# A graph network of two layers on one core: the last 13 blocks of the second layer as dense products, and one wait per chunk of gathers in the first

## The reference

```python
# first layer
h    = relu(layernorm(x))
ea   = edge_attr @ W_edge.T + b_edge            # (200000, 96)
msg  = relu(h[src] + ea)
aggr = segment_sum(msg, dst)                    # (6250, 96)
x    = x + relu(((1 + eps) * h + aggr) @ W1.T + b1) @ W2.T + b2
# second layer: a softmax over the edges of each target, per feature
h    = relu(layernorm(x))
m    = relu(h[src]) + 1e-7
a    = softmax of m over the edges with the same dst
out  = x + (h + segment_sum(a * m, dst)) @ W + b
```

## Time and profile before

| | |
|---|---|
| median of 3 runs | 3177.6 us (3171.68 to 3183.03) |
| the profiled execution, its own time | 3172.46 us |
| its span | 3170.7 us |
| mean granted clock of PE | 0.778 |
| PE busy | 2043.8 us (64%), 11221 matmuls |
| PE weight loads busy | 1635.3 us (52%) |
| DVE busy | 1922.5 us (61%) |
| ACT busy | 762.9 us (24%) |
| POOL busy | 1740.9 us (55%) |
| moved by DMA | 322.53 MB, mean 102 GB/s |
| gathers of the first layer (L564 into `rows_buf`) | 1563, mean 962 ns |
| idle of POOL ahead of them | 944.0 us |

### The profile page before, as it was taken

How to read it: one execution, slowest core, us unless ns; L and a number is a source line. 1 busy time by engine, 2 the same in 40 slices (tenths; PEclk the granted TensorE clock), 3 DMA queues, 4 the chain that set the end, 5 groups by cost and what they waited for, 6 DMA issues and landing times.

```text
span 3170.7 us, 45342 instructions
## 1 busy us (share of the span) xinstructions
PE 2043.8 (64%) x11221; PEld 1635.3 (52%) x11222; DVE 1922.5 (61%) x4523; ACT 762.9 (24%) x1322; POOL 1740.9 (55%) x1820
## 2 busy tenths in 40 slices
PE   3466666666666666666656676666666674777778
PEld 1255555555555555555545555555555563455556
DVE  7466666666666666666666666666667871233334
ACT  4000011112222222333333333334343550000000
POOL 5356666566666666666666666666666104444441
PEclk8677777777777777777787777777777876788889
DMA  4122333333333333334333343332222155455443
GB/s 134 22 59 70 81 76 79 79 89 93 91 87 94 94 105 96 98 99 108 107 100 105 107 115 103 109 105 71 62 62 62 39 161 175 158 164 164 162 162 119
DMA packets 152071, 322.53 MB, mean 102 GB/s; under 512 B 65291, under 2 KB 106027, under 8 KB 137791
## 3 DMA queue, kind: packets, MB, share of 16 engines
q1 hardware_dynamic: 27286, 151.94, 16.2%
q0 software_dynamic: 61632, 100.73, 13.9%
q10 hardware_dynamic: 63014, 68.51, 6.4%
HBM read 247.64 MB, written 73.38 MB: 101 GB/s over the span
## 4 chain that ended last, share of the span: by engine, by line
DVE 27%; PE 21%; another core or an unknown queue 21%; issue 18%; DVEq 6%; ACT 1%; DMA 0%; SPq 0%; ACTq 0%
DVE zone L1369 14%; PE ps L849 11%; DVE planes L1140 5%; DVE ps L1341 5%; PE ps L775 4%; PE ps L659 3%; DVEq L1369 2%; PE ps L859 1%; DVEq L374 1%; PE ps L646 1%; DVE planes L1146 1%; PE ps L680 1%; DVE features_buf L1354 1%; DVE onehot L1140 1%
## 5 line engine op out<-in xcount | busy, mean ns | idle before, releaser
L564 POOL DMA_INDIRECT rows_buf<-table,index x1563 | 1503.0, 962 | 944.0 <-remote 426.0
L775 PE MATMUL ps<-zone,planes 128*128 128x400 f16 x2352 | 682.7, 411 | 852.2 <-DVE zone L1369 662.3
L775 PEld LDWEIGHTS ps<-zone,planes 128*128 128x128 f16 x2352 | 268.4, 114 | 1036.2 <-issue 976.7
L992 ACT ACTIVATE features_buf<-ps 128x800 f16<-128x800 f32 x392 | 328.2, 837 | 1696.3 <-PE ps L775 829.7
L1369 DVE TENSOR_SCALAR zone<-iota_c,planes 128x400 f16<-128x400 int16 x2352 | 686.0, 345 | 56.2 <-issue 52.1
L659 PEld LDWEIGHTS ps<-wet,zone 128*128 128x128 f32 x3136 | 625.0, 279 | 49.2 <-issue 45.2
L659 PE MATMUL ps<-wet,zone 128*128 128x96 f32 x3136 | 601.0, 358 | 0.0
L1341 DVE TENSOR_TENSOR ps<-ps,rows_buf 128x768 f32<-128x768 f32 x195 | 187.5, 962 | 494.1 <-remote 447.2
L646 PE MATMUL ps<-onehot,features_buf 128*96 128x128 f32 x3120 | 478.9, 305 | 1.5 <-issue 1.5
L646 PEld LDWEIGHTS ps<-onehot,features_buf 128*96 128x96 f32 x3120 | 446.6, 193 | 20.9 <-issue 7.8
L1140 DVE TENSOR_TENSOR onehot<-ps,dstf 128x1024 f32<-128x1024 f32 x196 | 239.1, 1220 | 228.8 <-remote 224.8
(11 more groups left out here) (184 smaller groups left out, 778.6 us busy)
## 6 DMA issues: line engine op xcount, KB each, us to landing
zone<-edge_t SPq DMA_DIRECT2D x98, 768.0 KB
counts<-features_buf ACTq DMA_DIRECT2D x288, 200.0 KB
rows_buf<-counts SPq DMA_DIRECT2D x24, 1600.0 KB
rows_buf<-table,index POOLq DMA_INDIRECT x1563
planes<-counts SPq DMA_DIRECT2D x12, 1600.0 KB
table<-planes SPq DMA_DIRECT2D x5, 840.0 KB
final<-residual ACTq DMA_DIRECT2D x48, 48.0 KB
out<-final ACTq DMA_DIRECT2D x48, 48.0 KB
```

The lines of the kernel that those rows point to most:

```text
L564: nc.gpsimd.indirect_dma_start(out=into[:, t, :], out_offset=None, in_=table, in_offset=bass.IndirectOffsetOnAxis(ap=at[:, t:t + 1], axis= ...
L775: nc.tensor.matmul(count_ps[:, bass.ds(banks[k], WC)], row_hot[:, u % 2, g * GS + k, :], pair_hot[:, g * GS + k, :], start=False, stop=Fal ...
L992: nc.scalar.activation(count_out[:, k], bank, ACT.Copy, accum_out=row_sum[:, bass.ds(p, 1)]).then_inc(moved, 1)
```

## The change

Three things are changed together.

1. `ORDER`, `FETCH` and all of the fetched path go: the loads of edge ends, the gathers, the one-hots, `fetched_sums`, the stores of the weighted table (L500), and the part of the checks that bounds the edges of the fetched blocks. All 49 blocks are `block_sums`, in order.
2. ACT's `close` stores all 392 pairs of counts, 104 more stores of 200 KB; its wait for the last four stores moves to the end of the loop.
3. `chunk_rows` issues the 8 gathers of a chunk behind one wait, `ea_done, c - 6`. The waits for `add_done` and `sum_done` go.

Cut to its core:

```diff
-LOTS = [range(0, 3), range(3, 6), range(6, 8)]
...
-DB = 36
-GB = NB - DB
-FETCH = [20, 20, 20, 19, 19, 19, 19, 19, 18, 18, 18, 18, 15]
-FETCH_AT = [sum(FETCH[:g]) for g in range(GB + 1)]
-LEAD = 6
-ORDER = []
-for d in range(DB):
-    ORDER.append(d)
-    ORDER.extend(DB + g for g in range(GB) if LEAD + 5 * g // 2 == d + 1)
-assert len(ORDER) == NB
-EPAD = P * max(FETCH)
...
-                def weighted_store(u):
-                    wait_high(sp, u)
...
-                sp.wait_ge(starts_ready, 1)
-                for g, start in enumerate(load(sp, block_start, DB, GB, [E] * GB)):
-                    n = FETCH[g]
-                    sp.dma_start(fetch_ends[:, :, FETCH_AT[g]:FETCH_AT[g] + n],
-                                 edge_ends[:, bass.ds(start, P * n)].rearrange("e (p k) -> p e k", k=n)
-                                 ).then_inc(fetch_in, 16)
...
                 for u in range(NU - 2):
                     own_store(u)
-                weighted_store(0)
-                weighted_store(1)
-                own_store(NU - 2)
-                weighted_store(2)
-                own_store(NU - 1)
+                for u in range(NU - 2, NU):
+                    own_store(u)
                 block_load(2)
-                weighted_store(3)
                 sp.wait_ge(own_out, 2 * NU * 16)
                 sp.wait_ge(step_done, SC + NSTEP)
                 for b in range(2):
                     sp.dma_start(own[:, b, :], own_rows[b * P:(b + 1) * P, :]).then_inc(residual_in[b], 16)
-                weighted_store(4)
-                for b in range(3, DB):
-                    sp.wait_ge(block_ps, 2 + ORDER.index(b - 3) + 1)
+                for b in range(3, NB):
+                    sp.wait_ge(block_ps, b)
...
-            def rows_of(u, tiles):
-                gather(rows[:, u % RS], table0, index[:, u % IS], rows_in[u % RS], tiles)
-
-            def chunk_rows(i, u, lots=LOTS):
+            def chunk_rows(i, u, paced=True, tiles=T):
                 c = i * IS + u
-                pool.wait_ge(add_done, c + 1)
+                if paced:
+                    pool.wait_ge(ea_done, c - (RS - 2))
                 if u % RS == 0:
                     pool.wait_ge(index_in[u % IS // RS], (i + (u // IS + 1)) * 16)
                 pool.sem_inc(gathers_begun, 1)
-                rows_of(u, lots[0])
-                if len(lots) > 1:
-                    pool.wait_ge(ea_done, c - (RS - 2))
-                    pool.sem_inc(gathers_begun, 1)
-                    rows_of(u, lots[1])
-                    pool.wait_ge(sum_done, c + (NS + 1 - RS))
-                    pool.sem_inc(gathers_begun, 1)
-                    rows_of(u, lots[2])
+                gather(rows[:, u % RS], table0, index[:, u % IS], rows_in[u % RS], tiles)
 
             pool.wait_ge(table_out, 2 * NU * 16)
             for u in range(RS):
-                chunk_rows(0, u, [range(T)])
+                chunk_rows(0, u, False)
             with pool.Fori(0, (NC - RS) // IS) as i:
                 for u in range(RS, RS + IS):
                     chunk_rows(i, u)
             for u in range(RS + (NC - RS) // IS * IS, NC - 1):
                 chunk_rows(0, u)
-            chunk_rows(0, NC - 1, [range(T_END)])
+            chunk_rows(0, NC - 1, tiles=T_END)
...
-            with pool.Else():
-                pool.wait_ge(fetch_in, GB * 16)
-                pool.wait_ge(own_out, 2 * NU * 16)
-                pool.wait_ge(weighted_out, 2 * NU * 16)
-                for g in range(GB):
-                    if g >= 2:
-                        pool.wait_ge(block_ps, 2 + ORDER.index(DB + g - 2) + 1)
-                    gather(fetched[g % 2], weighted, fetch_ends[:, 0, FETCH_AT[g]:FETCH_AT[g + 1]], fetched_in[g % 2],
-                           range(FETCH[g]))
...
-                    pe.wait_ge(bad_ready, 3)
-                    nc.tensor.transpose(ps[0:1, 6, 0:P], bad[:, 2:3], ident[:, :])
-                    nc.tensor.matmul(ps[0:1, 6, P:P + NB], ones[:, 0:1], in_block[:, :], start=True, stop=True)
-                    nc.tensor.matmul(ps[0:NB, 7, 0:1], in_block[:, :], ones[:, 0:1], start=True, stop=True).then_inc(bad_ps, 1)
-                if g == 3:
-                    pe.wait_ge(edges_moved, 1)
-                    nc.tensor.matmul(ps[0:1, 5, 0:NB], block_edges[:, :], upper[0:NB, 0:NB], start=True, stop=True
-                                     ).then_inc(starts_ps, 1)
...
-                def fetched_sums(s, g):
-                    pe.wait_ge(fetched_in[g % 2], fetched_before(g + 2))
-                    pe.wait_ge(fetch_hot_done, g + 1)
...
-                    if ORDER[s] < DB:
-                        block_sums(s, ORDER[s])
-                    else:
-                        fetched_sums(s, ORDER[s] - DB)
+                    block_sums(s, s)
...
-            def close(p, k, needed, kept):
+            def close(p, k, needed):
 
                 bank = count_ps.rearrange("p (b c) -> p b c", b=CB)[:, PW * (k % PB):PW * (k % PB + 1), 0:WC]
                 act.wait_ge(step_done, at_least_zero(act, needed, SC + NSTEP))
-                if kept:
-                    act.wait_ge(stored[k], p * (16 // OB) + (16 - k * (16 // OB)))
+                act.wait_ge(stored[k], p * (16 // OB) + (16 - k * (16 // OB)))
                 nc.scalar.activation(count_out[:, k], bank, ACT.Copy,
                                      accum_out=row_sum[:, bass.ds(p, 1)]).then_inc(moved, 1)
                 act.wait_ge(moved, p + 1)
                 nc.scalar.activation(bank, zeros[:, :].rearrange("p (w c) -> p w c", w=1).to_broadcast([P, PW, WC]),
                                      ACT.Copy).then_inc(cleared, 1)
-                if kept:
-                    act.dma_start(counts[:, bass.ds(p * PW, PW), :], count_out[:, k]).then_inc(stored[k], 16)
+                act.dma_start(counts[:, bass.ds(p * PW, PW), :], count_out[:, k]).then_inc(stored[k], 16)
 
             act.wait_ge(table_out, 2 * NU * 16)
             act.wait_ge(filled, 5)
             act.wait_ge(first_clear, 1)
             act.wait_ge(meta_ready, 1)
-            with act.Fori(0, KEPT // OB) as i:
+            with act.Fori(0, NPAIR // OB) as i:
                 needed = load(act, ready, i * OB, OB, [SC + NSTEP] * OB)
                 for k in range(OB):
-                    close(i * OB + k, k, needed[k], True)
+                    close(i * OB + k, k, needed[k])
             for k in range(OB):
-                act.wait_ge(stored[k], (KEPT // OB + 1) * 16)
-            with act.Fori(KEPT // OB, NPAIR // OB) as i:
-                needed = load(act, ready, i * OB, OB, [SC + NSTEP] * OB)
-                for k in range(OB):
-                    close(i * OB + k, k, needed[k], False)
...
-            nc.vector.tensor_reduce(in_block[:, :], row_sum[:, :].rearrange("p (b k) -> p b k", b=NB), AX.X, ALU.add
-                                    ).then_inc(bad_ready, 1)
             dve.wait_ge(bad_ps, 2)
             chain(nc.vector.tensor_reduce(bad[0:1, 3:4], ps[0:1, 6, 0:P], AX.X, ALU.max))
-            chain(nc.vector.tensor_tensor(block_over[:, :], ps[0:1, 6, P:P + NB], block_room[:, :], ALU.subtract))
-            chain(nc.vector.tensor_reduce(most_over[:, :], block_over[:, :], AX.X, ALU.max))
             chain(nc.vector.tensor_scalar(good[0:1, 1:2], bad[0:1, 3:4], COUNT_MAX, good[0:1, 0:1], ALU.is_le,
                                           ALU.mult))
-            chain(nc.vector.tensor_scalar(good[0:1, 2:3], most_over[:, :], 0.0, good[0:1, 1:2], ALU.is_le, ALU.mult))
-            nc.vector.tensor_copy(fast[:, :], good[0:1, 2:3]).then_inc(fast_ready, 1)
-            nc.vector.tensor_copy(block_edges[:, :], ps[0:NB, 7, 0:1]).then_inc(edges_moved, 1)
...
-                def fetch_places():
-                    dve.wait_ge(fetch_in, GB * 16)
...
-                def fetch_hots(g):
-                    dve.wait_ge(fetch_at_ready, g + 1)
-                    if g >= 2:
-                        dve.wait_ge(block_ps, 2 + ORDER.index(DB + g - 2) + 1)
-                    for k in range(FETCH[g]):
```

More of the change, by code:

```diff
@@ L97 @@
 assert NPAIR == SB and NPAIR % OB == 0
-KEPT = DB * BW // PW
-assert KEPT % OB == 0
 MW = 20
@@ L246, in gnn_kernel @@
         table16 = planes[:, 0:NJ * 2 * D].bitcast(F16).rearrange("p (j d) -> p j d", j=NJ)
-        fetched = [buf[:, 0:max(FETCH) * 2 * D].bitcast(F16).rearrange("p (k d) -> p k d", d=4 * D)
-                   for buf in (zone, features_buf)]
-        fetch_hot = [buf.bitcast(F16)[:, 0:max(FETCH) * P].rearrange("p (k n) -> p k n", n=P)
-                     for buf in (onehot[:, :, :, :].rearrange("p a b c -> p (a b c)"), dstf[:, :])]
         blocks = [buf.bitcast(F16) for buf in (planes[:, NJ * 2 * D:NJ * 2 * D + BW * WC // 2],
@@ L350, in gnn_kernel @@
         block_ps = sem("block_ps")
-        edges_moved = sem("edges_moved")
-        starts_ps = sem("starts_ps")
-        starts_ready = sem("starts_ready")
-        fetch_in = sem("fetch_in")
```

(43 more changed lines are left out.)

35 lines of the change are left out of this document (6 added, 29 removed).

## The result

The changed kernel took 3133.7 us (median of 4 runs, 3132.74 to 3136.37), the kernel before 3178.5 in the same comparison: ratio 0.9862, 95% interval 0.9843 to 0.9881. Forecast were 3,023 and a range of 2,985 to 3,110. The profiled execution took 3133.81 us.

A forecast was written before the change was run, and what follows sets the result against it. No engine was full; PE's signals, late while POOL gathers, were taken as the bound. Terms −143.9 − 10.5 + 0 = −154.4 us from the median of 3,177.6 gave 3,023 us, range 2,985 to 3,110.

The forecast's parts named there:

- All blocks dense, −143.9: Second layer's blocks: without gathers, steps from block 2 to the last fall from 540.6 to 396.7 us, −143.9 us.
- The second rival: Second layer's blocks: gathers are not why signals are late, so dense blocks add matmul time, 3,233 us; chance 0.04.
- The start, −10.5: Start of the blocks: without the weighted table's stores, block 2 begins at about 2612.5 instead of 2623.02, −10.5 us.
- Loads of blocks: Second layer's blocks: loads at 211 GB/s keep up with dense blocks of 8.44 us; no cost.
- 104 more stores, 0: ACT's added stores of counts after its closes: hidden, 0 us; 35 us in all if that cover were gone.
- One wait per chunk, 0: First layer's loop: POOL already runs eight gathers between waits, so the period stays 12.37 us; 0 us.
- the rival: First layer's loop: double runs of 16 gathers, 29.6 us per two chunks against 24.7; chance 0.06 for deciding.
- a part of it: First layer's loop: double runs in some pairs only, which leaves a gain, 3,045 to 3,160 us; chance 0.13.

The follow-up runs named there:

- z1: The changed kernel with the three lots and three waits of before in the gathers, dense blocks kept; on chip 8: 2994.2 us, ratio 0.9521.
- z6: The changed kernel with a second wait, for the sums, in the same place ahead of a chunk's eight gathers; on chip 12: 3043.8 us, ratio 0.9694.

## Why the forecast was wrong, step by step

- *All blocks dense, −143.9.* From block 2's start to the end of the last product, 540.6 became 3124.41 − 2728.11 = 396.3: −144.3. Right. It holds where signals are late; on chip 3 this term has the other sign. The second rival, +55 us in all, is what chip 3 shows (+54), from a cause that I hadn't thought of: the gathers do make the signals late, but not on every chip.
- *The start, −10.5.* −11.1. Right. *Loads of blocks*: no block waited. Right. By the Trainium skill ("TensorE: Matmul & The Clock Gate", section "The cost: per-tile semaphore tail") the increments of PE's matmuls serialize at some 26 ns each; with no gather beside it, the trace agrees (0.04 us), and beside a run of gathers it does not (10.35 us).
- *104 more stores, 0.* On chip 3 the loop's last add came at 2028.9 us before and at 2024.7 after; on chip 8, z1 has these stores and came within 4.4 us of the forecast for everything but the single wait. Right.
- *One wait per chunk, 0.* **This step failed**: +116.4 here, +121 alone on chip 8. I argued that POOL already stood before eight gathers in the period shown, and that the next edge signal would again come after the run. That was true of the period shown, and still is of 144 of the 188 periods. What I left out is every eighth chunk, in which POOL pauses 1.1 us though the profile shows nothing that it waits for. The signal can then get through inside the run; a double run follows in 19 of 23 such chunks. With one wait POOL then runs on; a second wait, for the sums, holds it (z6). The trace before shows no such pause, so it could not have been read off. But the rival had its price right: 29.6 us a pair forecast, 29.69 measured. That it came so close is in part luck. In the pair shown, the sixteen gathers and the pause take 20.54 us instead of 19.7 and the late signal 3.02 instead of 1.77, while DVE's next add follows the release after 5.10 us instead of 7.4. I gave a part of it a chance of 0.13 and 3,045 to 3,160 us, and then ended the range at 3,110, about halfway. Had it reached to that case's own bound, it would have held the time.

## What to carry to other kernels

A wait that never seems to bind can be the cap on a rare case. Before several waits are merged into one, ask of each what it would stop if the others were passed early, and price that event, not the period in which it does nothing. And a gain that rests on one effect (here late signals) is only as general as the effect. The same edit gave ratios of 0.9862 and 0.9938 where signals were late, and on a chip without late signals it cost 2.3%.

## What the runs showed of the hardware

- The kernel before took 3139 to 3179 us in four comparisons, on chips 8 and 12 among others, and 2459 on chip 3. The busy times of POOL and DVE hardly differ (POOL 1740.9 and 1757.4 us, DVE 1922.5 and 1895.5); the waits do. What makes signals late there, and why not on chip 3, no run tells.
- Where signals are late, they come through in the first part of a run of gathers and are held in the rest, up to 14 us in the double run above (890.82 − 876.68). With a stand of about 1 us after the first gather they can come through later in the run, 7.3 us after its start in the double run above (874.56 − 867.26).
- "Late signals" is a name for what the rows show, and perhaps too narrow a one. The ends of matmuls in the profile are modelled, so a product that really ends late looks the same. And PE's own work is held as well: these are products of one dense block of the kernel before, the one that begins at 2832.09 in the earlier trace rows. None of them has a wait, and they run beside the gathers:

```profile
2836.63 0.65 PE L849 MATMUL ps<-planes,rows_buf 125*128 125x384 f16 x3 [1.13 <-issue]
...
2845.10 0.48 PE L849 MATMUL ps<-planes,rows_buf 125*128 125x384 f16 x1 [1.71 <-issue]
```

- The first 64 gathers of both kernels run without a wait. The first add comes at 162.3 us (before) and 162.1 (after) in the first comparison, and at 110.1 and 108.8 on chip 3. The kernel before in that stretch, first with late signals, then on chip 3 (PE is busy 27.53 and 60.67 us of 85.50):

```profile
35.50:121.00 85.50, 27.53 (x122) 12.51 (x120) 37.61 (x91) 18.31 (x28) 65.74 (x64) 0.63 0.17 37
```

```profile
35.50:121.00 85.50, 60.67 (x297) 35.33 (x296) 76.82 (x176) 21.45 (x34) 68.11 (x57) 0.84 0.17 33
```

So this run of gathers costs up to 52 us where signals are late, an estimate from these two starts. The change leaves it as it is.
- POOL stands 1.11 us after the 49th of every 64 gathers, on chips 8 and 12, where that gather is the first after a wait. In the kernel before and in z1, where it is not, no such pause is found.
